# Five products of zeros at the start of a convolution kernel are left out

## The reference

```python
t1 = p1_w * x
t2 = x + t1
t4 = relu(x)
t5 = unfold(x, 3, 7)                      # 21 shifted copies of x
t7 = einsum('oc,nchw->nohw', p7_w, t4)
t8 = unfold(t7, 1, 5, dilation 3)         # 5 shifted copies of t7
t9 = x[:, :, None] - t8
t10 = einsum('ngihw,goi->ngohw', t2 in 4 groups, p10_w in 4 groups)
t11 = einsum('nck,nmk->ncm', t1, t5) / sqrt(h * w)
t12 = t9.mean(2)
t13 = einsum('ncm,nmk->nck', t11, t10) / sqrt(c * 21)
out = maximum(t13, t12)
```

## Time and profile before

| | |
|---|---|
| median of 3 runs | 389.93 us (389.7 to 390.0) |
| the profiled execution | 389.44 us |
| its span, from the first to the last instruction | 387.6 us |
| TensorE busy (matmuls) | 382.1 us, 99% |
| VectorE busy | 327.7 us, 85% |
| ScalarE busy | 254.3 us, 66% |
| GpSimd busy | 89.2 us, 23% |
| DMA | 88.80 MB, 229 GB/s |

### The profile page before, as it was taken

How to read it: one execution, slowest core, us unless ns; L and a number is a source line. 1 busy time by engine, 2 the same in 40 slices (tenths; PEclk the granted TensorE clock), 3 DMA queues, 4 the chain that set the end, 5 groups by cost and what they waited for, 6 DMA issues and landing times.

```text
span 387.6 us, 10235 instructions
## 1 busy us (share of the span) xinstructions
PE 382.1 (99%) x4024; PEld 169.8 (44%) x4024; DVE 327.7 (85%) x401; ACT 254.3 (66%) x721; POOL 89.2 (23%) x77
## 2 busy tenths in 40 slices
PE   7999999999999999999999999999999999999996
PEld 3223563335633365333743338333383334732382
DVE  7899899899798896888978887889968889688645
ACT  3424479779567755677477772676827768277790
POOL 1534312221222202222022220222202222222300
PEclk9999999999999999999999999999999999999999
DMA  8999486494977556794767937779377683553115
GB/s 301 397 348 409 163 296 213 138 316 133 323 259 267 197 200 218 256 330 125 220 222 265 334 114 257 229 261 326 120 243 257 247 274 111 178 178 109 56 57 216
DMA packets 28704, 88.80 MB, mean 229 GB/s; under 512 B 3312, under 2 KB 3824, under 8 KB 28656
## 3 DMA queue, kind: packets, MB, share of 16 engines
q1 hardware_dynamic: 28656, 88.14, 66.0%
HBM read 71.35 MB, written 16.78 MB: 227 GB/s over the span
## 4 chain that ended last, share of the span: by engine, by line
PE 98%; DVE 0%; issue 0%; DVEq 0%
PE ps_y L830 43%; PE ps_y L929 13%; PE ps_t L852 12%; PE ps_p L852 12%; PE ps_y L841 9%; PE ps_t L929 2%; PE ps_y L852 1%; PE ps_y L1074 1%; PE ps_p L1012 1%; PE ps_t L830 1%; PE ps_y L977 1%; PE ps_p L830 1%; PE ps_p L977 0%; PE ps_t L1012 0%; PE ps_t L841 0%
## 5 line engine op out<-in xcount | busy, mean ns | idle before, releaser
L830 PE MATMUL ps_y<-v_planes,u_planes 64*64 64x512 f32 x1488 | 183.4, 594 | 0.6 <-issue 0.4
L306 POOL TENSOR_TENSOR t1T<-t1T,p1T_sb 128x512 f32<-128x512 f32 x64 | 82.3, 1308 | 266.8 <-PE ps_y L841 236.2
L414 ACT ACTIVATE t<-xn,p_plus 128x64 f32<-128x64 f32 x512 | 127.9, 334 | 0.0
L852 PE MATMUL ps_t<-t,aT 64*64 64x512 f32 x440 | 113.0, 590 | 0.1
L852 PE MATMUL ps_p<-box,p_fifth 64*64 64x512 f32 x424 | 108.8, 589 | 0.0
L830 PEld LDWEIGHTS ps_y<-v_planes,u_planes 64*64 64x64 f32 x1488 | 55.0, 133 | 111.5 <-issue 105.6
L641 DVE STREAM_TRANSPOSE yT<-ps_y 128x512 f32<-128x512 f32 x62 | 40.7, 694 | 30.4 <-PE ps_y L841 30.4
L338 ACT ACTIVATE base<-ps_p 128x512 f32<-128x512 f32 x55 | 32.8, 597 | 47.5 <-PE ps_p L852 46.9
L929 PEld LDWEIGHTS ps_y<-t1T,yT 128*128 128x128 f32 x448 | 50.5, 192 | 5.7 <-issue 5.7
L929 PE MATMUL ps_y<-t1T,yT 128*128 128x128 f32 x448 | 51.9, 277 | 0.0
L675 DVE TENSOR_TENSOR base<-ps_t,base 128x512 f32<-128x512 f32 x56 | 38.4, 686 | 12.1 <-PE ps_t L852 11.8
(11 more groups left out here) (75 smaller groups left out, 219.2 us busy)
## 6 DMA issues: line engine op xcount, KB each, us to landing
xw<-x_conv SPq DMA_DIRECT2D x63, 561.0 KB, 6.6
xn<-x_nat SPq DMA_DIRECT2D x32, 512.0 KB, 4.5
t1T<-x_pix SPq DMA_DIRECT2D x32, 512.0 KB, 5.3
out<-base SPq DMA_DIRECT2D x63, 256.0 KB, 4.8
u_planes<-w_tiles SPq DMA_DIRECT2D x4, 336.0 KB, 5.7
out<-base SPq DMA_DIRECT2D x2, 128.0 KB, 2.1
p1T_sb<-p1T SPq DMA_DIRECT2D x1, 128.0 KB, 8.1
p_sb<-p7T SPq DMA_DIRECT2D x1, 64.0 KB, 8.2
```

Of the source, the lines that this page charges most:

```text
L306: nc.gpsimd.tensor_tensor(part, part, p1T_sb[:, e, :].unsqueeze(1).broadcast_to([P, 4, C]), ALU.mult).then_inc(t1_ready, 1)
L414: last = nc.scalar.activation(t2[:, h, W * r:W * (r + 1)], xn[:, f, at:at + W], ACT.Copy, scale=p1_plus[:, 8 * h + r:8 * h + r + 1])
L830: last = nc.tensor.matmul(dst[TILE * pair:TILE * pair + TILE, :], weights_of(rows_of(half), u, weights, TILE * k, TILE), data_of(rows_of(h ...
L852: last = nc.tensor.matmul(dst[cols, 0:data.shape[-1]], weights[rows, cols], data[rows, :], start=start, stop=False, skip_group_check=True)
```

## The change

The five products of zeros go, with the wait ahead of them and their semaphore p7_bank_set; the wait for that semaphore in seed_x goes too. The memsets of relu_pad are two, one for each whole buffer, instead of three. relu waits for both memsets before its first two uses.

```diff
-ZERO_ROWS = 7
-WARM = 5
-        p7_bank_set = sem("p7_bank_set")
...
                 act.wait_ge(xn_loaded[f], 16 * (n + 1))
+                if i < 2:
+                    act.wait_ge(zeroed, 2)
                 wait(act, box_steps, BOX_STEPS * (i - 1))
...
                 act.wait_ge(xn_loaded[h // 2], 16 * (n + 1))
-                act.wait_ge(p7_bank_set, WARM)
...
-            nc.vector.memset(relu_pad[:, 1, 0:ZERO_ROWS], 0.0).then_inc(zeroed, 1)
-            nc.vector.memset(relu_pad[:, 1, ZERO_ROWS:], 0.0).then_inc(zeroed, 1)
-            nc.vector.memset(relu_pad[:, 0], 0.0).then_inc(zeroed, 1)
+            for buffer in range(2):
+                nc.vector.memset(relu_pad[:, buffer], 0.0).then_inc(zeroed, 1)
...
-            pe.wait_ge(zeroed, 1)
-            zeros = relu_pad[:, 1, 0:ZERO_ROWS].rearrange("p a b -> p (a b)")
-            for bank_set in (ps_p7[:, 0:HALF // 2], ps_p7[:, 0:HALF // 2], ps_t13, ps_p7, ps_p7[:, 0:HALF // 2]):
-                nc.tensor.matmul(bank_set[:], zeros[:, 0:P], zeros[:, 0:bank_set.shape[-1]], start=True,
-                                 stop=True).then_inc(p7_bank_set, 1)
```

## The result

The changed kernel took 391.77 us, the median of 7 runs (390.65 to 393.17), beside 389.70 us (389.55 to 390.88, 7 runs) for the kernel before: ratio 1.0048, 95% interval 1.0034 to 1.0063. That is 1.9 us slower by the ratio, 2.07 us by the medians. In a second set of runs it was 391.74 us (390.94 to 392.78) beside 389.74, ratio 1.0049 (1.0037 to 1.0062). The forecast was 392.2 us, 2.25 us slower than 389.93.

What follows compares the result with a forecast made beforehand. The kernel was taken as bound by one TensorE stream of products from the first real one at 7.50 us; terms 0 + 0 + 0 + 2.25 us on the median 389.93 gave 392.2 us, range 391.0 to 394.1.

Steps and rivals of the forecast that it cites:

- What the zeros were for: TensorE's start: zeros run in otherwise idle time, and the clock rises during them, at 6.25 us.
- The first product: TensorE's first real product stays at 7.50 us, held by VectorE's 7.39 us; gain 0 to 0.1 us, taken as 0.
- The slow stretch: Unit 0's real products run at half rate until a rise 4.79 us after the first, at 12.29 us; delay 2.25 us.
- Where it goes: After unit 0: nothing on TensorE's path has slack, so all 2.25 us arrive at the end.
- A: Late rise: lower clock lasts into the second or third unit, delay 3.1 to 4.2 us, 393.1 to 394.1; chance 0.14.
- B: Early rise, 1.5 to 3.3 us after the first product: delay 0.75 to 1.6 us, 390.7 to 391.5; chance 0.14.
- C: Zeros slow for another cause than the clock; real products start at full rate, 389.8 to 389.9 us; 0.07 with D.
- D: The queue of first products also starts later, for want of something the zeros had done; chance 0.07 with C.

Runs made afterwards that it cites:

- a_again: The changed kernel run once more without any edit, for a second trace of its start: 391.74 us.
- e1_elsewhere: Changed kernel with five products of zeros put back, into a bank of unit 1, with no semaphore others wait for; first memset cut at row 7: 389.59 us.
- e7_four_zeros: Kernel before with only its first four products of zeros instead of five: 389.65 us, ratio 0.9993.
- e8_earlier_zeros: Kernel before with the first memset cut from 7 rows to 4 and seven 256-column products of zeros instead of five: 389.92 us, ratio 1.0005.
- e3_memsets_kept: Kernel before without its five products of zeros, three memsets kept, semaphore and waits as in the changed kernel: 391.76 us, ratio 1.0049.
- e2_early_three: Kernel before with only its first three products of zeros instead of five: 391.41 us, ratio 1.0049.
- e6_pool_half: Kernel before with four products of zeros and the second half of unit 0's V_1 made on GpSimd instead of VectorE: 390.04 us, ratio 1.0019.

## Why the prediction was right

**What the zeros were for.** The reading that they ran in idle time and that their work was the clock's rise is shown: the same stream of zeros elsewhere restores the time (389.59), its removal makes the whole loss with the memsets as before (391.76), the real loads go from 133 to 227 ns, and the clock's own records rise at 6.23 us before and at 10.12 and 12.94 after. What the prediction had wrong on the way is its sentence that the row of the clock and the durations disagree: the 1.00 over the zeros stands for time ahead of the first record. It went by the durations, and those were right.

**The first product.** Forecast at 7.50 with a gain of 0 to 0.1 us. It comes at 7.30 and 7.44 in the two traces, but the kernel before has it at 7.50 and 7.9: the landing of the first transfers spreads it over 0.6 us. Within that nothing of the change is to be seen. The memsets did not end at 3.04 us as I had it but at 3.39, as before: the first began at 1.04 us instead of 0.90, and the second still came at 2.32 after 0.20 us idle. It was hidden by the transfer, except in the first trace, where the weights had landed and VectorE started at 3.51.

**The slow stretch.** I took the one rise that the trace showed, 4.79 us after the first product, and worked out 2.24 us. Measured in the kernels without enough zeros: 2.8, 4.1, 5.5 and 5.6 us after the first real product, with losses in unit 0 of 1.38, 1.91, 2.59 and 2.62 us. The conversion from the one to the other holds: four rounds and their pause took 3.80 us slow (a_again) where the prediction had 11.24 - 7.50 = 3.74, and the slow k = 2 another 0.84. The mean loss of the three traces without any zeros is (1.38 + 2.59 + 1.91)/3 = 1.96 us, the medians say 2.0. The step is right and 4.79 lies within what happens; that 2.25 landed near 2.0 owes something to luck, since one trace gives one draw. How long the slow stretch is differs between executions of one program: the two traces of the changed kernel rose 2.8 and 5.5 us after the first product. Its 13 runs spread over 2.5 us. The kernel before lay within 0.3 us in its first three runs; of its 76 runs 70 lie within 1.2 us, the other six above.

**Where it goes.** Forecast: through to the end, nothing swallowed. The last column of the table shows it, 371.5 us from unit 2 in every kernel. What I had called a slip of VectorE "by a little less" is a second small bound: unit 2's first load waits for L578 in the changed kernel, 0.93 us idle against 0.84 before, and the distance from unit 1 to unit 2 is 4.51 and 4.63 us instead of 4.41. In these two traces that adds 0.1 to 0.2 us to the loss in unit 0. It is not special to the change: the kernel before has 4.51 in its second trace, and e1_elsewhere (4.67), e7_four_zeros (4.67) and e8_earlier_zeros (4.95) have it with a full-rate start. In the last three VectorE had waited 0.3 to 0.6 us for xw to land ahead of its planes, which fits a VectorE that falls behind.

**The rivals.** A, a rise in the second or third unit, is not seen in a trace: in all of them it was there by unit 0's 32x32 products. But one run in thirteen of the changed kernel, at 393.17 us, lies in A's range, and it was not profiled. Its span of 391.4 us less the fixed 371.5 puts unit 2 at 19.9 us, an estimate; the latest in a trace, with a unit 0 that was slow in all its 64x64 steps, is 19.14. So a rise in unit 1 is rare at most, and not excluded. B, an early one, was the profiled run itself (2.8 us, 390.65 us): rises differ within one kernel, and its case was a part of the spread and not an alternative. C falls with the 227 ns, D with the first product at 7.30 and 7.44 us. The view of the clock read 1.00 over the slow stretch, as foreseen, for the reason given in the section on the result.

## What to carry to other kernels

Look at what idle TensorE time before the first real product is filled with before it is cleared away: products that nobody reads can be what lets the real ones start at the full rate, here worth 2 us of 390. Read the level off the durations and spacings of one form of weight load and off the start of the trace's first clock record; the mean granted clock over a stretch ahead of that record read 1.00 here while the median load took 227 ns instead of 133. Look whether anything downstream has slack; if nothing has, as here, where 371.4 to 371.5 us followed unit 2's first load in all twelve traces, the end of the run can be read off after the first units. One trace gives one draw of such a start; take the size from several, and keep the filling products inside the idle time, since what overruns is paid (0.5 us in the trace here).

## What the runs showed of the hardware

- Ahead of the rise 64x64 weight loads took 227 ns in the changed kernel, 133 in the kernel before behind its rise, and rounds of products were 0.85 instead of 0.43 us apart. No trace of the twelve has a record of the clock ahead of the rise (4.78 to 13.45 us), and the view's mean over such a stretch read 1.00 (7.30:10.00 in the changed kernel); the start of that record agrees to within 0.1 us with each rise worked out above from the spacing of the loads.
- From the first real product without a rise before it to the full rate it took 2.8 and 5.5 us in two executions of one program (the changed kernel), and 4.1 and 5.6 in two near variants (e3_memsets_kept, e2_early_three). Zeros that began at 1.46 us rose at 5.42, 5.55, 5.58, 6.09, 6.23 and 6.67 us, those that began at 1.22 at 4.78. After the rise idle pieces of 1.2 (e7_four_zeros) and 1.67 us (e6_pool_half) did not lower the clock again; three products at the lower level, followed by a pause of 2.65 us, were no help (391.41 us, e2_early_three).
- The kernel before is perhaps not quite safe from a late rise either: 6 of its 76 runs in all sets lie above 390.5 us, up to 394.95. Whether these are late rises was not seen, as none of them was profiled, and earlier zeros did not remove such runs. Ten runs have a mean granted clock of 0.996: three of e2_early_three, four of e6_pool_half, one each of e7_four_zeros and e8_earlier_zeros, and the one at 394.95. In the traces the mean falls below 1.00 only by a fall just before the end of the span (to half at 387.07 us of 388.1 in e8_earlier_zeros, mean 0.999), so it does not show when the rise was. It stays open.
- One VectorE addition of 64x544 took 1.75 us beside a GpSimd addition of the same size that took 1.81 us, against 0.73 us alone.
